# Third layer of a four-layer model: each of the second half's sixteen row scatters waits for one first expert tile

## What is computed

```
attention:  q, k, v = split(xn @ W_qkv.T + b_qkv)            one head, causal, 128 wide
            s = softmax(mask(q @ k.T) / sqrt(128)) @ v
experts:    24 experts, four groups of 256 tokens, capacity C per expert and group
            logits = xn @ Wg;  gates = softmax(logits)
            idx1, idx2 = the two best experts of a token
            loc1, loc2 = running count of a token within its expert's queue
            combine = g1 * onehot(expert1, loc1) + g2 * onehot(expert2, loc2), dropped where loc >= C
            h   = relu(layer_norm(combine @ (dispatch(xn) @ W1 + b1), per-group weights))
            f   = layer_norm(combine @ (dispatch(h) @ W2 + b2) + xn)
```

## Time and profile before

| What | us |
|---|---|
| Median of 3 runs | 2050.77 |
| Lowest, highest | 2050.46, 2055.49 |
| The profiled execution's own time | 2040.68 |
| Its span from first to last instruction | 2038.9 |
| PE, DVE, ACT, POOL busy in the span | 1716.2, 1462.0, 1139.9, 284.5 |
| The 32 row scatters of the change, first start to last start | 1097.9 to 1137.7 |

### The profile page before, as it was taken

One profiled execution on the slowest core, in us unless ns is written; L12 is line 12 of the kernel. 1 busy time (PEld: TensorE's weight loads), 2 busy tenths in 40 slices (PEclk: granted clock), 3 DMA queues, 4 the chain that ended last, 5 costly groups with the idle time before them and its releaser, 6 DMA issues. The chain is left out here.

```text
span 2038.9 us, 44089 instructions
## 1 busy us (share of the span) xinstructions
PE 1716.2 (84%) x17561; PEld 819.0 (40%) x17561; DVE 1462.0 (72%) x2798; ACT 1139.9 (56%) x2246; POOL 284.5 (14%) x394
## 2 busy tenths in 40 slices
PE   4699999999999986799987787783579999999967
PEld 2222222232232224344435445672324444555546
DVE  5889999999999925855566036435878888899725
ACT  3278888888888881322212333342216676777744
POOL 1000000000000000000003244323012222211123
PEclk8799999999999997999987889787759999999988
DMA  4011112211111021052323387641410111111032
GB/s 137 32 55 62 49 49 73 65 54 48 66 50 36 3 47 65 3 127 84 92 84 127 104 289 248 206 112 39 176 53 26 36 34 35 30 29 28 13 86 79
DMA packets 78037, 154.52 MB, mean 76 GB/s; under 512 B 18684, under 2 KB 35964, under 8 KB 74136
## 3 DMA queue, kind: packets, MB, share of 16 engines
q1 hardware_dynamic: 63152, 121.57, 19.1%
q0 software_dynamic: 14384, 29.29, 4.6%
q10 hardware_dynamic: 296, 0.85, 0.1%
HBM read 102.23 MB, written 48.89 MB: 74 GB/s over the span
## 5 line engine op out<-in xcount | busy, mean ns | idle before, releaser
L785 ACT ACTIVATE heads_probs<-heads_pS 128x512 f32<-128x512 f32 (+3 forms) x1664 | 857.9, 573 | 233.9 <-PE heads_pS L664 211.1
L808 DVE TENSOR_REDUCE heads_run_max<-heads_pM 128x1 f32<-128x1024 f32 x512 | 598.9, 1219 | 50.2 <-PE heads_pM L686 47.8
L664 PE MATMUL heads_pS<-heads_qs,heads_ks 75*32 75x512 bf16 (+3 forms) x6656 | 598.3, 372 | 17.4 <-ACT heads_probs L785 14.6
L726 PE MATMUL heads_pO<-heads_probs,heads_vh 128*32 128x512 f32 (+2 forms) x3328 | 437.6, 571 | 3.2 <-ACT heads_probs L785 1.4
L664 PEld LDWEIGHTS heads_pS<-heads_qs,heads_ks 75*32 75x32 bf16 x6656 | 185.9, 95 | 319.1 <-ACT heads_probs L785 170.1
L664 PE MATMUL heads_pM<-heads_ks,heads_qs 72*32 72x512 bf16 (+3 forms) x2560 | 274.9, 370 | 14.1 <-DMA heads_qs<-k_parts_dram 8.4
L819 DVE TENSOR_REDUCE heads_run_max<-heads_pM 128x1 f32<-128x512 f32 x384 | 247.7, 685 | 30.3 <-PE heads_pM L664 27.7
L686 PE MATMUL heads_pM<-heads_ks,heads_qs 64*128 64x512 bf16 x512 | 182.8, 394 | 44.2 <-DVE heads_run_max L808 29.7
L572 POOL DMA_DIRECT2D k_head_out_dram<-heads_ot x120 | 62.6, 529 | 880.8 <-DVE heads_ot L842 644.6
L686 PE MATMUL heads_pM<-heads_kd,heads_qd 64*128 64x512 bf16 x512 | 182.9, 394 | 0.0
L1507 DVE TENSOR_REDUCE second_row_max<-second_banks 128x1 f32<-128x2048 f32 (+15 forms) x16 | 20.7, 1291 | 168.1 <-PE second_banks L1465 118.1
(11 more groups left out here) (375 smaller groups left out, 2016.0 us busy)
## 6 DMA issues: line engine op xcount, KB each, us to landing
top_weights<-k_comb_dram SPq DMA_DIRECT2D x128, 128.0 KB, 3.0
second_w<-in_L_W_dram SPq DMA_DIRECT2D x12, 1024.0 KB, 9.3
k_hid_slots_dram<-k_zeros SPq DMA_DIRECT2D x8, 1152.0 KB, 4.7
k_h_slots_dram<-second_work SPq DMA_DIRECT2D x48, 192.0 KB
second_work<-k_hid_slots_dram SPq DMA_DIRECT2D x48, 192.0 KB
k_parts_dram<-proj_part SPq DMA_DIRECT2D x12, 512.0 KB, 4.0
heads_qs<-k_parts_dram SPq DMA_DIRECT2D x64, 96.0 KB
heads_ks<-k_parts_dram SPq DMA_DIRECT2D x60, 96.0 KB
```

Source lines behind the costliest of these rows:

```text
L664: mm = pe.matmul(out[cols, :], still[:, cols], moving, start=start, stop=stop)
L726: mm = pe.matmul(pO[k * 32:k * 32 + VW, int(second), o:BLK], vh[c][:, t, :], probs[u % 2][:, k * BLK + o:(k + 1) * BLK], start=first_chunk ...
L785: act.activation(probs[u % 2][:, k * BLK + c0 - b * BLK:(k + 1) * BLK], pS[:, slot, 0:c1 - c0], ACT.Exp)\
L808: dve.reduce_max(run_max[:, i, blocks[0][0] // 2:blocks[0][0] // 2 + 1], both.rearrange("p k c -> p (k c)"), AX.X).then_inc(taken, 2)
```

## The change

POOL's function `scatter_x` gets one wait in front of each of the second half's sixteen scatters: the first waits for `opened` to be 1, the next for 2, and so on to 16. `t` runs from 8 to 15 and `c` from 0 to 1, so the value is 1 to 8 for the first choice and 9 to 16 for the second. Nothing else is changed, and no other stream differs.

```diff
             def scatter_x(k):
                 for c in range(2):
                     for t in range(HALF_TILES * k, HALF_TILES * (k + 1)):
+                        if k == 1:
+
+                            pool.wait_ge(opened, 1 + HALF_TILES * c + t - HALF_TILES)
                         pool.indirect_dma_start(
                             out=K.x_slots[k], out_offset=bass.IndirectOffsetOnAxis(ap=K.place_i[:, c, t:t + 1], axis=0),
                             in_=K.xn[:, t, :], in_offset=None).then_inc(x_scattered[k], 16)
```

## The result

| | before | changed |
|---|---|---|
| Median of 4 runs, us | 2050.61 | 2030.28 |
| Lowest, highest | 2046.63, 2055.49 | 2029.26, 2034.73 |
| The profiled execution | 2040.68 | 2029.48 |
| PE, DVE, ACT, POOL busy | 1716.2, 1462.0, 1139.9, 284.5 | 1711.5, 1461.3, 1137.6, 283.9 |

The profiled executions differ by 11.2, of which 1.0 lies ahead of the first scatter. The changed kernel's profiled execution is one of its four runs; that of the kernel before is none of its four.

The account below looks back on a forecast made before the run. PE's completions were taken to arrive late in attention beside POOL's unbroken line of indirect DMAs. Terms -11.3 - 3.3 - 1.9 + 3.9 + 2.6 = -10.0 took 2050.8 to 2040.8 us; 8-in-10 range 2032 to 2057.

Parts of the forecast that it names:

- the last of the sum: Whole kernel: the timed median's 10.1 us above the profiled execution carried over unchanged, turning 2030.7 into 2040.8 us.
- first late hand-over: ACT's copy at the end of the first sixteen scatters, 2.6 us late: expected to stay, gain 0, other bound -2.6.
- second, third and the clock: Attention steps 1 and 2: two late hand-overs vanish, -11.3 and -3.3 us; PE at full clock, -1.9 us.
- all up to tile 0: Attention up to the first expert tile: late hand-overs removed and PE's clock restored, -11.3, -3.3 and -1.9 us.
- late hand-overs beside tiles: Expert tiles beside the moved scatters: one late hand-over at the line's end, +2.6 us, lower bound 0.
- SP's wait: SP's load_x(6) waits for moved scatters, delaying tile 15's store and ACT's copy of tile 19: +3.9 us, bounds +2.1, +5.4.
- the dear end of the clock: Attention: the bound of PE's gain from running at full clock, -3.1 us where -1.9 was taken.
- a case of 0.05: Later attention steps meet the gathers at other moments and lose a small gain again; chance 0.05.
- Rival 1: Late hand-overs exist only in profiled executions; timed runs keep just the +3.9 us wait on SP: 2054.7 us, chance 0.2.
- Rival 2: In attention the slots' first loads, not POOL's line, make hand-overs late, so these stay: 2054.7 us, chance 0.13.
- Rival 3: Lateness moves with the scatters to the expert tiles and costs more there: +22.6 us, 2073.4 us, chance 0.12.
- Rival 4: POOL reaches the new waits later than the tiles anyway, so they do nothing; excluded for the first, no chance given.

Follow-up runs that it names:

- r5: The changed kernel without further edit, on chip 0: 2025.56 us against 2044.59 for the kernel before, ratio 0.9909.
- r11: The kernel before without the second half's sixteen scatters, slot loads kept, on chip 11: 2029.43 us, ratio 0.9908 to the kernel before.
- r12: The changed kernel with SP's loads 6 and 7 behind the store of tile 17 instead of 14, chip 11: 2034.09 us, ratio 0.9940 to before.
- r14: The kernel before with turns of two groups in attention steps 1 and 2 made four times, chip 11: 2058.64 us, ratio 1.0052 to before.
- r13: The kernel before with the second half's sixteen scatters all waiting for the first tile alone, chip 11: 2039.50 us, ratio 0.9960.
- r2: The kernel before with the second half's sixteen scatters all waiting for the first tile alone, chip 13: 1965.47 us, ratio 1.0030.
- r7: The kernel before with the second half's sixteen scatters all waiting for the first tile alone, chip 8: 1965.13 us, ratio 1.0029.

## Why the prediction was wrong, and in what it was right

**The step that failed** is the last of the sum: "The median of the timed runs is 10.1 above that execution; I take the difference over as it is." Between the two profiled executions the sum held: 2030.7 forecast, 2029.48 measured. But the offset was no constant. Before, the profiled execution lies 9.9 below the median of 2050.61, and below every one of the four timed runs; for the changed kernel the profiled one is 0.8 below its median. On chip 11 nine runs of before lie between 2044.0 and 2050.2, and leaving the second line out brings 18.5; on chip 0 the change brings 19.0. So a gain of 18 to 20 is the usual one, and the pair of recordings, with 11.2, compared an execution of before shorter than all its four timed runs with an ordinary one of the change. On chip 0 three of nine runs of before are as short (2037.6 to 2039.1), so such executions do occur. I had the sign of this in hand, and used 10.1 us of unexplained time as a mere offset, with no bounds of its own in the range, when the same late hand-overs that I was removing were the first candidate to vary. That they are what varies is my inference. One comparison fits it: the two recordings of the changed kernel end at 931.8 and 928.4 after `place_i`, and their late hand-overs sum to 55.9 and 50.9. But no longer execution of before was recorded where hand-overs are late, so where its further 10 us lie stays open.

The terms of the sum, against the profiled executions:

| term | forecast | measured |
|---|---|---|
| first late hand-over | 0 | 2.6 us late, now 2.1: -0.5 |
| second, third and the clock | -16.5 | |
| all up to tile 0 | -16.5 | 55.7 to 37.9 after place_i: -17.8 |
| late hand-overs beside tiles | +2.6 | tiles 0 to 15 from 17.5 to 20.1: +2.6 |
| SP's wait | +3.9 | tiles 15 to 19 from 4.6 to 7.1: +2.5 |
| sum at tile 19 | -10.0 | -12.7 |
| gather(0), then gather_y | no change | -13.7, then -8.2 |
| end | -10.0 | -10.2 |

- *Up to tile 0.* Both hand-overs went, and the clock is 1.00 where it was 0.53. The 1.3 us more than forecast are about the 0.5 above and the dear end of the clock (-3.1 in place of -1.9 would be 1.2).
- *Beside the tiles.* The size was right, the form not: not one hand-over late by 2.6 at the end of the line, but two in its middle, 2.0 us at tile 9 and 2.7 at tile 10 (and 0.2 at tile 8), of which PE, a tile ahead, hid a part. That both came to 2.6 is luck.
- *SP's wait.* A store landed in 3.1 us, as I took it (midway between 1.3 and 4.6 would be 2.95). But I added two terms that overlap: the line took 20.8 us, 1.3 longer than the 19.5 I used, while the tiles lost 2.6, so the tiles' own delay covers 1.3 us of SP's: 3.9 - 1.3 = 2.6.
- *Later.* From gather(0) to gather_y 5.5 us are given back. Late hand-overs there sum to 29.4 us against 26.9, and 4.1 against 3.2 in the stretch before. r5, r11 and r12 give back 2.1, 6.3 and 5.0 us there, and these amounts don't go with their sums of late hand-overs, so what gives it back is not shown. I had this as a case of 0.05 ("gain a little and lose it in later steps of attention"); it belonged in every case. At the end -10.2, which makes my -10.0 partly luck: -12.7 at tile 19, and 2.5 lost behind it.

**Rival 1** (profiled executions only) is wrong in its number: the timed runs won more than the profile. Its idea is not out. Every timed run lists its span and clock too, so each seems to have been recorded. And the recordings with late hand-overs are the ones that lack records (136 of 512 for the 32 scatters), in the same stretches, so a recorder that can't keep up on some chips would fit what is seen. Whether an execution that nobody records has late hand-overs, and so whether the change wins anything there, is not shown. **Rival 2** fell with r11: POOL's line left out, loads kept, lateness gone. The rule that I set beside it (page "SBUF — State Buffer" of the Trainium skill, section "Who interferes with whom": DMA never contends with a compute engine) would have given no gain. On the five chips of the fast kind the runs agree with it; on the others POOL's indirect DMAs and PE's completions don't keep apart (11.4 us, 24.0 in r14), and the measurement decides. It does not show that the rule itself fails, for the traces do not tell whether the DMA, POOL itself, the recording or something else delays them. **Rival 3** was real as a mechanism but held down by the pacing; unpaced it costs 8.7 us more (r13). **Rival 4**: after the first, two of fifteen waits bound, and on such chips these two may be what keeps rival 3 small.

And one question that I didn't ask: on which chip? The change gains 0.9% where hand-overs are late (the result's chip and chip 0) and loses 0.4% where they are not (chip 8; r2 and r7, with one wait, lose 0.3%). The kernel that lost on neither is r12's (0.9940 where late, 1.0000 and 1.0006 where not), at a third less gain.

## What to carry to other kernels

When an engine begins long after the last thing it needs has ended, and it does so beside a long unbroken line of indirect DMAs from POOL, break the line or move it away from the dense stretch, and let each DMA wait for a step of the work it stands beside: sixteen tiles took 20.1 us so, against 28.8 with one wait. Look before that at whether one program takes the same time on different chips. Where waits vary from one execution to the next, an offset between the profiled execution and the median is not a constant: it is the first place to look for more, or less, of the very effect that is being removed. And terms that delay the same instruction overlap; add up only what is left of the later one after the earlier.

## What the runs showed of the hardware that I had not expected

- The same program takes 1960 us on five chips and 2037 to 2055 on two or three. Up to `place_i`, near 1097, they agree within 3.2 us. After it they part by 85.3 us, only while POOL issues indirect DMAs, and late hand-overs of PE account for most of that. Where POOL issued only direct DMAs, nothing is late by over 0.2 us.
- With 24 more matmuls a step beside the line hand-overs were 8.9 and 24.0 us late (r14), where before they were 0.04 and 2.6, with 11.4 the longest. The last ones end some 5 us behind the line: 1142.4 after POOL's last start at 1136.9, 1142.6 after 1137.7 in the kernel before.
- What is late is the change of PE's semaphore, not the engine that waits for it. The packed trace of before holds the times of these changes: the turn that ends at 1121.90 shows in its semaphore at 1133.24, and ACT begins 0.02 us later. The changes by ACT and DVE in the same stretch, as far as they are recorded, come 0.01 us after their instructions. PE's own rows go on in time, so the busy time of no engine rises (PE 1716.2 against 1711.5), and only the idle time before single instructions tells of it. The ends of PE's rows are modelled by the profile, so that PE had truly ended is likely, not certain.
- On the same chips records of semaphore changes are missing beside POOL's indirect DMAs (136 of 512 are left for the 32 scatters), and not in the stretches between.
